# Eight slots for the exponentials, four weighted sums of values in one bank, and another written-out order, in two attention layers on one core

## The reference, cut to what matters

```python
# layer 0 (emb: one vector of 512 per sequence)
xn = ln(x); q = softmax(xn@Wq + bq, over a head's 32 features); k = softmax(xn@Wk + bk, over tokens)
att = k^T v ; y = q att                                   # per head, 32x32
scale, shift = split(silu(emb)@W_emb + b_emb)
x = x + silu(ln(y)*(1+scale) + shift) @ W_out + b_out
# layer 1
q, k, v = xn@q_w + q_b, ...                               # xn = ln(x), 16 heads of 16
att = softmax(q k^T + mask, over keys)                    # 256 x 256 per head
y = att v
x = x + silu(ln(y)*(1+scale) + shift) @ out_w + out_b
```

## Time and profile before

| what | value |
|---|---|
| median of three runs | 807.55 us |
| the profiled execution, its own time | 807.33 us |
| its span, first to last instruction | 805.6 us |
| granted TensorE clock, mean share | 0.985 |
| instructions | 29123 |

### The profile page before, as it was taken

The page is one execution under the profiler, slowest core; times in us unless marked ns, Lnnn a source line. Parts: engine busy times, 40 slices in busy tenths (PEclk is TensorE's granted clock), DMA queues, the critical chain, the costliest instruction groups (busy, mean ns, idle before and its releaser), DMA issues. The chain is left out here.

```text
span 805.6 us, 29123 instructions
## 1 busy us (share of the span) xinstructions
PE 772.6 (96%) x10431; PEld 538.0 (67%) x10431; DVE 710.9 (88%) x1392; ACT 701.6 (87%) x1658; POOL 681.8 (85%) x1085
## 2 busy tenths in 40 slices
PE   7999889999999999999999999999999999999985
PEld 3575765777777677777677767777677776656542
DVE  7698899999999899998899889999889989989953
ACT  2266768899999999999999999999999999999995
POOL 7379998989999999998899998998989988897334
PEclk8799999999999999999999999999999999999998
DMA  6423544444443544355653445444544363354301
GB/s 179 91 48 80 139 115 117 103 104 121 101 125 95 126 110 105 88 146 100 126 127 92 132 89 123 111 109 89 143 115 120 72 119 91 85 148 115 110 20 53
DMA packets 149283, 86.22 MB, mean 107 GB/s; under 512 B 87404, under 2 KB 141802, under 8 KB 149130
## 3 DMA queue, kind: packets, MB, share of 16 engines
q1 hardware_dynamic: 149140, 84.36, 43.1%
HBM read 39.64 MB, written 25.80 MB: 81 GB/s over the span
## 5 line engine op out<-in xcount | busy, mean ns | idle before, releaser
L1301 DVE TENSOR_REDUCE NM<-banks 128x4 f32<-128x1024 f32 x256 | 306.7, 1213 | 23.3 <-PE banks L832 21.0
L1783 ACT ACTIVATE wraw<-banks 128x1024 f32<-128x1024 f32 x154 | 157.2, 1038 | 8.5 <-PE banks L845 7.7
L1985 POOL TENSOR_TENSOR rs<-ve,nhalf 128x2 f32<-128x2 f32 x128 | 89.8, 703 | 32.9 <-ACT ve L1656 31.7
L1783 ACT ACTIVATE PX<-banks 128x1024 f32<-128x1024 f32 x102 | 104.0, 1034 | 5.5 <-PE banks L845 4.6
L832 PE MATMUL banks<-SK,SQ 51*128 51x256 f16 x1024 | 96.1, 272 | 3.6 <-DMA SK<-scr 1.2
L701 PE MATMUL banks<-wo,SH 128*128 128x256 f16 x768 | 95.5, 274 | 4.2 <-POOL SH L2073 4.2
L845 PE MATMUL banks<-SQ,SK 53*128 53x256 f16 x1024 | 96.8, 272 | 1.7 <-DVE NM L1301 1.1
L701 PE MATMUL banks<-wv,ZT 128*128 128x256 f16 x768 | 95.3, 275 | 0.9 <-DVE un L1436 0.8
L2073 POOL TENSOR_TENSOR SH<-ST,SH 128x512 f16<-128x512 f32 x64 | 74.5, 1166 | 23.7 <-ACT SH L1747 20.0
L858 PE MATMUL banks<-wraw,V 128*32 128x256 f32 x1232 | 87.7, 385 | 0.7 <-ACT PX L1783 0.3
L2010 POOL TENSOR_TENSOR ZHL<-Z,ZHL 128x256 f16<-128x256 f32 x128 | 83.1, 670 | 2.6
(11 more groups left out here) (187 smaller groups left out, 1782.8 us busy)
## 6 DMA issues: line engine op xcount, KB each, us to landing
scr<-AB SPq DMA_DIRECT2D x64, 256.0 KB, 2.6
X<-in_x_dram SPq DMA_DIRECT2D x32, 256.0 KB, 3.0
SQ<-scr SPq DMA_DIRECT2D x64, 128.0 KB, 2.8
SK<-scr SPq DMA_DIRECT2D x64, 128.0 KB, 2.9
out_dram<-wemb SPq DMA_DIRECT2D x32, 256.0 KB, 2.6
SQ<-scr SPq DMA_DIRECT2D x64, 64.0 KB, 2.8
SK<-scr SPq DMA_DIRECT2D x64, 64.0 KB, 3.0
wemb<-in_L_cond_W_emb_dram SPq DMA_DIRECT2D x1, 1024.0 KB, 5.3
```

The lines of the kernel that those rows point to most:

```text
L1301: V.tensor_reduce(NMe[:, c, :, 2 * g:2 * g + 2], banks[:, n:n + 2, :].rearrange("p a (h m) -> p a h m", m=T), AX.X, ALU.max, negate=True). ...
L1783: A.activation(px(v % 5), banks[:, n:n + 2, :].rearrange("p a n -> p (a n)"), ACT.Exp, scale=r_uu).then_inc(S["exp"])
L1985: G.tensor_tensor(rs[:, b % 2, l, :], ve[:, b % 2, l, :], nhalf[:, :], ALU.pow).then_inc(S[f"r{l}"])
```

## The change

1. Slots 5 and 6 of the exponentials are laid on `wemb1`, slot 7 on `worw`. Part u of every sequence goes to slot u. `exp` waits for the part eight before. In sequence 0, part 5 waits also for `fx1` and `fm1`, part 7 for `wl_o0` and `wl_o1`.
2. Four `pv` parts share one bank, the first pair in columns 0 to 255 and the second in columns 256 to 511. One `yt` copies all 512 columns, so there are two per sequence instead of four, and the bank is waited for twice per sequence instead of four times.
3. The lists of all five queues, and with them `BANK`, `FREED` and `SETUP`, are new. They hold the same pieces but for the 64 `yt` that go.

```diff
-        px = lambda n: PX[:, n] if n < 3 else PX2[:, n - 3]
+        PX3 = wemb1[:, :, :].rearrange("p k n -> p (k n)").rearrange("p (i n) -> p i n", i=2)
+        PX4 = worw[:, :, :, :].rearrange("p l k n -> p (l k n)")
+        px = lambda n: PX[:, n] if n < 3 else PX2[:, n - 3] if n < 5 else PX3[:, n - 5] if n < 7 else PX4
 # pv
-                n = home(f"gpv{g}", b)
+                n, q = home(f"gpv{g // 2}", b), (g % 2) * T
-                if c == 0:
-                    clear(e, f"gpv{g}", b)
+                if u % 4 == 0:
+                    clear(e, f"gpv{g // 2}", b)
-                    m = PE.matmul(banks[32 * j:32 * j + 32, n, 0:T], V1[:, r, c, 4 * g + j, :],
-                                  px((8 * b + u) % 5)[:, at_px(j):at_px(j) + T], start=(c == 0), stop=(c == 1))
+                    m = PE.matmul(banks[32 * j:32 * j + 32, n, q:q + T], V1[:, r, c, 4 * g + j, :],
+                                  px(u)[:, at_px(j):at_px(j) + T], start=(c == 0), stop=(c == 1))
 # ty
-                e.wait_ge(S["yt"], 4 * b + 4)
+                e.wait_ge(S["yt"], 2 * b + 2)
 # exp
-                e.wait_ge(S["pv"], up(v - 4))
+                e.wait_ge(S["pv"], up(v - 7))
+                if u == 5:
+                    first(e, b, "fx1", "fm1")
+                if u == 7:
+                    first(e, b, "wl_o0", "wl_o1")
-                A.activation(px(v % 5), banks[:, n:n + 2, :].rearrange("p a n -> p (a n)"), ACT.Exp,
+                A.activation(px(u), banks[:, n:n + 2, :].rearrange("p a n -> p (a n)"), ACT.Exp,
 # yt
-                e.wait_ge(S["pv"], 8 * b + 2 * g + 2)
+                e.wait_ge(S["pv"], 8 * b + 4 * g + 4)
-                A.activation(YT[:, g, :], banks[:, home(f"gpv{g}", b), 0:T], ACT.Identity).then_inc(S["yt"])
+                A.activation(YT[:, 2 * g:2 * g + 2, :].rearrange("p g t -> p (g t)"), banks[:, home(f"gpv{g}", b), :],
+                             ACT.Identity).then_inc(S["yt"])
 # the lists around sequence 0, after: ACT
+            qt(5); th0(3); n1(4); at_(5); n0(7); sh0(3); ke(6); kt(6); qa(2); ka(2); at_(6); n2(3); th0(4); exp(0, 0)
+            n1(5); sh0(4); exp(0, 1); qe(6); n0(8); ke(7); exp(0, 2); qt(6); exp(0, 3); ka(3); exp(0, 4); exp(0, 5)
+            exp(0, 6); qa(3); n2(4); kt(7); yt(0, 0); wh_o1(); at_(7); exp(0, 7); th0(5); yt(0, 1); ke(8); sh0(5)
 # DVE
+            max_(2, 3); Y0(6); wl_o1(); max_(2, 4); qm(7); s0(9); km(8); rk(7); st0(5); vt(3); a0(9); rd_(0)
 # banks of rows(2, 0) and rows(2, 1), after, are free with exp:6 and exp:7
 # SP, after, begins
+            ld_c(); x_in(0); ld_m(); ld_w0(); ld_o0(); x_in(1); x_in(2); mbd0(); ld_r(); am(0); ld_f0(); z0T(0); am(1)
 # the end of ACT's list, before and after
-            exp(31, 7); yt(31, 0); yt(31, 1); yt(31, 2); yt(31, 3); sh1(29); th1(30); n3(31); sh1(30); th1(31)
-            sh1(31)
+            exp(31, 6); exp(31, 7); n3(30); yt(31, 0); yt(31, 1); sh1(29); th1(30); n3(31); sh1(30); th1(31); sh1(31)
...
```

More of the change, by code:

```diff
@@ L29 @@
     "ghot": "0",
[L30 to L42, removed]
+    "gcnd": "1",
+    "gt_w0": "1",
+    "gpm": "0",
+    "ga_w0": "1",
+    "gbb0": "2",
+    "grow3": "3",
+    "gbb1": "4",
+    "gt_o0": "1",
+    "gfx0": "5",
@@ L65 @@
[L65 to L87, removed]
@@ L1175, in _ @@
+            pv(31, 2); pv(31, 3); cols(31, 7); pv(31, 4); pv(31, 5); pv(31, 6); pv(31, 7); ty(31); y1T(30); o1(29)
+            y1T(31); o1(30); o1(31)
         @block.vector
@@ new lines, in _ @@
+            exp(6, 2); n3(5); exp(6, 3); qt(12); n1(11); exp(6, 4); kt(13); ka(9); exp(6, 5); qa(9); exp(6, 6)
+            yt(6, 0); exp(6, 7); th1(5); n2(10); at_(13); sh1(5); yt(6, 1); th0(11); sh0(11); qe(13); exp(7, 0)
+            exp(7, 1); n0(15); ke(14); exp(7, 2); qa(10); exp(7, 3); kt(14); n1(12); qt(13); n2(11); ka(10); exp(7, 4)
+            yt(7, 0); exp(7, 5); n3(6); exp(7, 6); at_(14); exp(7, 7); n1(13); th0(12); th1(6); n0(16); yt(7, 1)
+            sh0(12); sh1(6); exp(8, 0); ke(15); exp(8, 1); exp(8, 2); qe(14); exp(8, 3); exp(8, 4); kt(15); qt(14)
@@ new lines, in _ @@
+            exp(10, 6); exp(10, 7); at_(17); th0(15); th1(9); n0(19); sh0(15); yt(10, 1); ke(18); sh1(9); exp(11, 0)
+            exp(11, 1); ka(14); exp(11, 2); qa(14); qe(17); n3(10); exp(11, 3); n1(16); kt(18); exp(11, 4); qt(17)
+            exp(11, 5); exp(11, 6); n2(15); yt(11, 0); exp(11, 7); at_(18); th1(10); qe(18); yt(11, 1); sh1(10)
+            n0(20); th0(16); exp(12, 0); n1(17); ke(19); sh0(16); exp(12, 1); qt(18); ka(15); kt(19); exp(12, 2)
+            exp(12, 3); qa(15); exp(12, 4); n3(11); exp(12, 5); exp(12, 6); yt(12, 0); exp(12, 7); at_(19); n2(16)
@@ new lines, in _ @@
+            qe(19); yt(12, 1); th1(11); th0(17); n1(18); sh1(11); ke(20); qt(19); n0(21); sh0(17); exp(13, 0)
+            exp(13, 1); exp(13, 2); exp(13, 3); ka(16); kt(20); qa(16); n3(12); exp(13, 4); exp(13, 5); exp(13, 6)
+            yt(13, 0); exp(13, 7); th1(12); n2(17); sh1(12); exp(14, 0); th0(18); yt(13, 1); at_(20); n0(22); n1(19)
+            exp(14, 1); exp(14, 2); sh0(18); exp(14, 3); qe(20); ke(21); ka(17); n3(13); qt(20); kt(21); exp(14, 4)
+            qa(17); exp(14, 5); n2(18); exp(14, 6); exp(14, 7); yt(14, 0); th1(13); th0(19); yt(14, 1); sh1(13)
@@ new lines, in _ @@
+            exp(17, 0); sh0(21); kt(24); exp(17, 1); n1(22); qt(23); exp(17, 2); ka(20); n3(16); exp(17, 3)
+            exp(17, 4); qa(20); exp(17, 5); n2(21); exp(17, 6); exp(17, 7); yt(17, 0); th0(22); th1(16); yt(17, 1)
+            n0(26); sh1(16); exp(18, 0); exp(18, 1); sh0(22); ke(25); qe(24); n1(23); at_(24); exp(18, 2); ka(21)
+            exp(18, 3); qa(21); qt(24); exp(18, 4); n3(17); exp(18, 5); yt(18, 0); exp(18, 6); n2(22); exp(18, 7)
+            kt(25); qe(25); th1(17); at_(25); th0(23); exp(19, 0); yt(18, 1); exp(19, 1); sh1(17); exp(19, 2); sh0(23)
```

986 lines of the change are left out of this document (452 added, 534 removed), and 67 rows, old and new, of the table FREED.

## The result

| | before | after |
|---|---|---|
| median of the timed runs (9 each, lowest to highest) | 808.41 us (807.31 to 809.95) | 804.73 us (800.39 to 806.29) |
| profiled execution, and its span | 807.33 us | 800.39 us, 798.6 us |

The ratio is 0.9947 [0.9924, 0.9971]: faster by 0.5%, 4.3 us of 808.4. The forecast was 801.4. Later the changed kernel was timed again beside other kernels: 803.50 us, ratio 0.9912 [0.9881, 0.9944]. Together the two intervals allow 2.3 to 9.6 us. An execution more than 1.5% above the fastest of its kernel is left out of a ratio, which happened once, to the profiled one of experiment 10.

The account below looks back on a forecast made before the run. ACT sets the pace in the middle (94.8% busy), DVE and POOL close behind. Terms -2.9 - 1 - 3 + 0.8 = -6.1 us from 807.33 give 801.2, with 0.2 to the median 801.4; range 793 to 811.

Parts of the forecast that it names:

- ramp: Start of the kernel: the reordered preparation was given 0, with 2 us either way.
- gate: Sequence 0: `exp(0, 7)` now waits for `wl_o1`, most of it filled by ACT's work; +0.8 us, bounds 0 and +2.8.
- tail: From the last exponential to the end: latency, fewer copies but `n3(30)` before them; 0.
- The copies: ACT: one 512-column copy for two of 256 saves 3.8 us, three quarters reaching the end; -2.9 us, bounds 0 and -5.1.
- The handoffs: ACT's copies: 64 waits for `pv` go, each new copy needs four `pv`; -1 us, bounds -2.1 and +2.1.
- Rival C: Slower by the wait of `exp(0, 7)` for `wl_o1`: a 7 us stop, about 811 us; chance 0.21.
- The slots and the order: Slots alone worth nothing; longer PE cover takes a quarter of ACT's 12.2 us waits; -3 us, bounds -12 and +5.
- sign of proof: ACT's idle time in 200 to 700 us falls from 25.9 to some 22, before line 1783 down from 10.1.
- A: The new order gives much more: ACT's idle time in the middle halves, -13 us, some 791.5; chance 0.15.
- B: Nothing arrives: ACT's saving turns into idle time before `cols` and layer-1 products; 807.3 us; chance 0.14.

Follow-up runs that it names:

- experiment 10: The changed kernel with twelve extra matmuls of 512 columns in the preparation, results unused: 800.23 us, ratio 0.9894 to the kernel before.
- experiment 1: The changed kernel with each copy of 512 columns split into two of 256 again: 804.62 us, ratio 0.9928 to the kernel before.
- experiment 8: The changed kernel with slot 7 in memory of its own and no wait of `exp(0, 7)` for `wl_o1`: 802.81 us, ratio 0.9930 to the kernel before.
- Experiment 5: The kernel before, with its own lists, banks and copies, given eight slots and `wl_o1` moved behind `Y0(6)`: 810.13 us, ratio 1.0020.
- experiment 2: The changed kernel, new lists and copies kept, with five slots and without the new waits in sequence 0: 812.53 us, ratio 1.0036 to the kernel before.
- experiment 7: The changed kernel with lists that begin with the first 100 us of the kernel before: 808.56 us, ratio 1.0003 to the kernel before.
- experiment 12: The kernel before with twelve extra matmuls of 512 columns in its preparation, results unused: 807.87 us, ratio 0.9986.
- experiment 4: The changed kernel timed and profiled again without an edit: 803.50 us, ratio 0.9912 to the kernel before; profiled execution 802.63 us.

## Why the prediction was right or wrong

The forecast was -6.1 us against the profiled execution. The two profiled ones differ by 6.9, the medians of the first comparison by 3.7. The direction and the range held. The terms did not all hold, and that the sum came within 1 us of the profiled pair is luck: 3.6 us of the 6.9 were won in the ramp, for which the forecast had 0 and a gate of +0.8, and the tail lost 1.5. In the second profile of after the ramp gives 0.2, the middle the same 4.1, and the whole is 4.7.

**The copies: the saving right, the share that arrives too large.** Forecast -2.9 of a saving of 3.8. The starts stand 0.49 to 0.51 us apart, forecast 0.48, and against two adjacent copies that saves 2.6 to 3.8. What was mis-sized is the three quarters that were to reach the end: it is 0.7 of 2.4 us in the middle, and at most 0.9 in the last seven sequences, where ACT is at 28.72 of 30 us. The 2.2 us by which experiment 1 is longer there would have made the sum 2.9, just the forecast, but 1.3 of them go with the half clock in sequence 30. This rests on one trace of each; the ratios of the two overlap. The Trainium skill (ScalarE: Activation LUTs, "What ACT_TABLE_LOAD costs") gave 0.52 us for 512 columns, near the 0.49 to 0.51 here, but 0.31 for 256, where the rows have 0.27 to 0.28. So the saving estimated by the Trainium skill, 5.9 us, was too large. It is not the time of one copy that is off: the rows have 0.38 to 0.39 and 0.60 us for the two sizes, where an estimate from the Trainium skill's figures gives 0.40 and 0.61. But the short copies overlap the next instruction by 0.10 to 0.12 us here, where the Trainium skill has 0.09.

**The handoffs: the waits shrank, what arrived is not shown.** Forecast -1. In 120:720 the idle time before the copies fell from 2.5 to 0.8 us. ACT's idle time over the 22 sequences stayed (26.6 and 26.5), and no run undoes the shared bank, so this term can't be told from the next.

**The gate: right in place, and worth less.** Forecast +0.8, by a stop at `exp(0, 7)` between 141 and 143 us. The stop is 0.72 us, at 138.2, since the ramp was earlier. In the trace of experiment 8, without it, the end comes no earlier. Rival C needed a stop of 7 us. Experiment 5 shows how much the list around the gate matters: there, in the old lists, the stop is 2.5 us.

**The slots and the order: the step that failed.** "The slots remove no wait that the trace shows, so by themselves they are worth nothing" is true of the old lists (experiment 5) and was the wrong question for the new ones. I gave the new lists -3 us by their longer cover, as if they could stand on five slots. On five they are 0.4% slower than before; on six or eight 0.5 to 0.9% faster. The longer PE work that I counted between `cols` and `pv` of part 5, 5.1 us after 3.7, fits this, since the stops with five slots stand at parts 5 and 6; that it is the reason is not shown. The wait for a slot was absent in before because its lists had been arranged around it, which the prediction says, and then prices at nothing. The term's size, -3, is near the middle's -4.1 less the 0.7 of the copies, which has the handoffs in it too. But its sign of proof failed: ACT's idle time was to fall from 25.9 to some 22, and it is 25.8. The waits that more cover was to shrink, 12.2 us before exponentials and copies, are 11.0 + 1.3 = 12.3. By the windows of equal work, slots and lists together bring 3.4 us without the new copies (before to experiment 1): 1.6 of ACT's busy time and 1.8 of its idle time. The idle time fell before the layer-1 products and not before the exponentials, first in before, then in experiment 1, over the 22 sequences:

```profile
L1763 ACT ACTIVATE R<-banks,fcs 128x256 f32<-128x256 f32 x88 | 43.3, 492 | 5.6 <-PE banks L709 5.1
```

```profile
L1757 ACT ACTIVATE R<-banks,fcs 128x256 f32<-128x256 f32 x88 | 43.1, 490 | 1.8 <-PE banks L703 1.3
```

These 3.8 us are more than the 1.8; smaller waits grew. Why the same 1124 or 1125 instructions keep ACT busy 1.6 us less is not shown.

**The ramp: a term I had at 0, with 2 us either way.** It moved by -4.6 at `exp(0, 0)` and -3.6 at `exp(2, 7)` in the first profile, by -0.3 and -0.2 in the second. The prediction had called itself wrong if the first exponential moved by more than 2 us, and in the first profile it did. The new preparation has `k0(0)` 4.1 to 4.2 us earlier in both. One thing that can be seen there is the condition's product, first before and then after:

```profile
24.53 6.38 PE L1002 MATMUL banks<-wemb,csT 128*32 128x512 f32 x8
```

```profile
21.53 5.10 PE L996 MATMUL banks<-wemb,csT 128*32 128x512 f32 x8
```

It starts 3.0 us earlier and, with less of it at half clock, takes 1.3 us less; the half clock of the preparation lasted 17.1 us in before (13.0 to 30.1) and 10.2 in after (14.3 to 24.5). By the other traces the clock has the larger part in this: where experiment 2 has 13.7 us of it `k0(0)` comes at 30.7 in the new order, where experiment 7 has as much it comes at 32.2 in the old one, and experiment 12 reaches it at 28.6 in the old order without any. What comes of it by the first exponential depends on the clock between 80 and 121 us, which differed between two executions of one kernel. The Trainium skill (TensorE: Matmul & The Clock Gate, "What's actually happening") says of a kernel's start that the number of matmuls at the lower clock differs from run to run of one kernel. Between the two traces of after the half clock near the start is as long, 10.2 us in both; what differs lies far behind it (0.98 and 0.92 in 40 to 120 us).

**The tail: forecast 0, in the profile +1.5.** 14.2 us from `exp(31, 7)` to `o(31)` became 15.7, with the clock at 0.71 in the last window. In the second profile it is 14.7, with the half clock from 796.6 us on only.

**The rivals.** A (791.5) is outside the measurement; ACT's idle time did not halve. B (nothing) was wrong as to the time, but its mechanism, that a saving on ACT turns into idle time, took 1.7 of the copies' 2.4 us in the middle. C didn't come about: the stop it needs is 7 us, and it is 0.72.

## What to carry to other kernels

Buffers and an order written out by hand are one thing. A buffer wait that a trace doesn't show may be absent because the order was found under it, so price a new order on the old number of buffers and on the new one, and count how far a reader lags before saying what a slot is worth. Compare stages at equal work, not in equal time windows: the window in us hid a gain of 4 us here. Before a difference of two traces is put down to the edit, look whether both have the same clock in that stretch: one stretch of 3.4 us at half clock near the end was worth 1.3 us here, more than the edit in the same stretch. And a gain in the ramp of a kernel whose preparation leaves TensorE at half clock for part of the time must be looked at in more than one execution.

## What the runs showed of the hardware

TensorE's granted clock falls to half also in the midst of work, and where it does so differs between executions of one program (83 to 121 us in one trace of after, nowhere there in the other). One such stretch at 766.3 us made a sequence of 11.4 us take 12.8 in experiment 1. In the first nine runs of after the time goes with the mean clock, from 0.977 at 806.0 to 806.3 us to 0.985 at 800.4 to 802.2, some 0.6 us per thousandth; in the six of experiment 4 it doesn't. The two traces of after have the lower clock only in the ramp and the tail. Twelve added matmuls of 512 columns in the preparation raised the mean clock of before, 0.981 to 0.987 without them, to between 0.985 and 0.996. Of the 4.8 us that they gave at the first exponential, nothing was left at the end (802.9 against 802.2).
